# A graph layer on 100,000 nodes: three more blocks are read again before the late scatters, and their late rows are patched in

## The reference, cut to what matters

```python
h = maximum(layernorm(x), 0)                     # x: 100000 nodes x 64
z = concatenate([h[src], h[dst], edge_attr], -1) # 25000 edges x 160
e = sigmoid(z @ W_f + b_f) * softplus(z @ W_s + b_s)
message = segment_sum(e, src, 100000)            # scattered sum into the nodes
mean, var = message.mean(0), message.var(0)      # over all nodes, per feature
normed = (message - mean) * rsqrt(var + 1e-5) * gamma + beta
out = x + h + normed
```

## Time and profile before

| what | value |
|---|---|
| runs | 1060.89, 1058.82 and 1062.35 us; median 1060.89 |
| profiled execution | 1058.33 us |
| its span, first to last instruction | 1056.6 us |
| busy, share of the span | PE 60%, DVE 69%, ACT 51%, POOL 69% |
| DMA over the span | 176.07 MB, mean 167 GB/s |

### The profile page before, as it was taken

One profiled execution on the slowest core, in us unless ns is written; L12 is line 12 of the kernel. 1 busy time (PEld: TensorE's weight loads), 2 busy tenths in 40 slices (PEclk: granted clock), 3 DMA queues, 4 the chain that ended last, 5 costly groups with the idle time before them and its releaser, 6 DMA issues. The chain is left out here.

```text
span 1056.6 us, 11040 instructions
## 1 busy us (share of the span) xinstructions
PE 633.3 (60%) x2470; PEld 454.9 (43%) x2470; DVE 733.0 (69%) x1544; ACT 539.4 (51%) x1178; POOL 731.9 (69%) x652
## 2 busy tenths in 40 slices
PE   0474666666556676655666666766656699944232
PEld 0242445454445464444454444544434589710000
DVE  2884675757575776756677665776766658799687
ACT  1263655555555565645466454664545564533332
POOL 6777777777777877777877777887878753240700
PEclk9865555555565555556555555655656679955555
DMA  8997535343434344243343424424333399899999
GB/s 316 400 383 290 126 77 124 83 119 94 108 96 106 75 87 86 56 86 58 83 87 55 86 61 81 85 56 86 70 71 60 30 353 404 297 308 427 413 405 376
DMA packets 88183, 176.07 MB, mean 167 GB/s; under 512 B 42575, under 2 KB 49299, under 8 KB 79699
## 3 DMA queue, kind: packets, MB, share of 16 engines
q1 hardware_dynamic: 35851, 115.32, 31.1%
q0 software_dynamic: 42880, 20.09, 16.0%
q10 hardware_dynamic: 9416, 40.29, 9.4%
HBM read 107.12 MB, written 68.53 MB: 166 GB/s over the span
## 5 line engine op out<-in xcount | busy, mean ns | idle before, releaser
L594 POOL DMA_INDIRECT m_buf<-in_x_dram,m_buf x384 | 367.2, 956 | 118.6 <-issue 109.1
L607 POOL DMA_INDIRECT msgs_dram<-sums,target x184 | 289.6, 1574 | 56.2 <-issue 55.8
L1171 PE MATMUL ps_all<-sums,m_last 128*128 128x64 f32 x920 | 189.4, 395 | 123.7 <-ACT m_last L1033 104.2
L1171 PEld LDWEIGHTS ps_all<-sums,m_last 128*128 128x128 f32 x920 | 181.9, 304 | 134.9 <-issue 110.8
L719 DVE TENSOR_REDUCE m_last<-late 128x24 f32<-128x1536 f32 (+1 forms) x49 | 85.3, 1741 | 87.8 <-ACT late L984 87.8
L1131 PE MATMUL ps_all<-ident,m_buf 128*128 128x128 f32 x192 | 53.2, 432 | 125.8 <-DVE m_buf L809 125.8
L1145 PEld LDWEIGHTS ps_all<-m_buf 128*128 128x128 f32 x392 | 92.1, 322 | 49.5 <-issue 49.5
L794 DVE TENSOR_TENSOR target<-moved,m_last 128x4 int32<-128x4 f32 x49 | 9.6, 196 | 146.5 <-POOLq L605 146.2
L1033 ACT ACTIVATE m_last<-m_last,one_col 128x512 f32<-128x512 f32 x196 | 107.6, 550 | 1.6
L1131 PEld LDWEIGHTS ps_all<-ident,m_buf 128*128 128x128 f32 x192 | 34.9, 217 | 158.2 <-DVE m_buf L809 137.3
L1143 PE MATMUL ps_all<-m_buf 128*128 128x512 f32 x98 | 99.8, 1121 | 0.0
(11 more groups left out here) (171 smaller groups left out, 1076.6 us busy)
## 6 DMA issues: line engine op xcount, KB each, us to landing
m_buf<-msgs_dram SPq DMA_DIRECT2D x38, 1024.0 KB, 12.1
m_buf<-in_x_dram SPq DMA_DIRECT2D x48, 512.0 KB, 5.0
msgs_dram<-y_kept SPq DMA_DIRECT2D x14, 1536.0 KB, 11.2
out_dram<-m_buf ACTq DMA_DIRECT2D x20, 1024.0 KB, 11.5
m_buf<-src_rows_dram SPq DMA_DIRECT2D x47, 256.0 KB, 4.1
y_spill_dram<-y_kept ACTq DMA_DIRECT2D x19, 512.0 KB, 2.8
y_kept<-y_spill_dram SPq DMA_DIRECT2D x8, 1024.0 KB, 12.8
m_buf<-in_x_dram,m_buf POOLq DMA_INDIRECT x392, 2.5
```

What stands on the lines that cost most here:

```text
L594: pool.indirect_dma_start(xg[:, n % G_SLOTS, 2 * j + c, :], None, x, bass.IndirectOffsetOnAxis(ap=ids[:, c, n * TILES + j:n * TILES + j + ...
L607: pool.indirect_dma_start(msgs, bass.IndirectOffsetOnAxis(ap=target[:, n % UNROLL, j:j + 1], axis=0), comb[:, n % COMB_SLOTS, j, :], None, ...
L1171: pe.matmul(ps_c[:, j, :], same_of(b, j, j + 1)[:, 0, :], msg_of(g)[:, b, :], start=(b == 0 and not begun), stop=(b == j), skip_group_chec ...
```

## The change

The three blocks behind the held ones (13, 14 and 15) are treated as the held ones are: their late rows are patched into `out` after their stores. For that

- `order` takes blocks 15 down to 10 after block 24, in place of 10 up to 15, so that blocks 15, 14 and 13 are positions 9, 10 and 11;
- `list_targets` counts a late row as one to be patched from block 13 on (`first_patched`), and makes a second list, `late_add`: such rows go to their dump row, the others to their target; the late scatters use this list;
- SP loads three y blocks ahead (`Y_AHEAD` = 3), then waits for the end of the scan on PE only, and issues the re-reads 0, 1 and 2; the wait for the late scatters and the rest rows stand before re-read 3. Y load 3 + k now follows re-read k;
- POOL waits for the stores of positions 0 to 11 before the patches, where it waited for 0 to 8.

```diff
-Y_AHEAD = 4
+Y_AHEAD = 3
+PATCHED = 3
@@ stage_one
+    at.dump_row, at.dump_late = dump_row, dump_late
@@ stage_two
+    late_add = keep("late_add", [P, LATE_TILES], I32)
+    to_dump = keep("to_dump", [P, LATE_TILES])
-    order = held + [NB - 1] + list(range(SPILLED_BLOCKS, NB - 1 - M_BUFS)) + list(range(SPILLED_BLOCKS))
+    order = held + [NB - 1] + list(range(SPILLED_BLOCKS, NB - 1 - M_BUFS))[::-1] + list(range(SPILLED_BLOCKS))
-    first_held = BLOCKS[held[0]][0]
+    first_patched = BLOCKS[held[0] - PATCHED][0]
@@ sync
-        sp.wait_ge(late_added, 16 * LATE_TILES)
-        sp.wait_ge(block_crossed, M_BUFS + 2)
-        sp.dma_start(m_rest[:, :], msgs[P * N_ROWS:NODES, :]).then_inc(rest_loaded, 16)
+        sp.wait_ge(block_crossed, NB)
         for k, i in enumerate(in_ring[M_BUFS:]):
+            if k == PATCHED:
+                sp.wait_ge(late_added, 16 * LATE_TILES)
+                sp.dma_start(m_rest[:, :], msgs[P * N_ROWS:NODES, :]).then_inc(rest_loaded, 16)
             r0, n = BLOCKS[order[i]]
             sp.wait_ge(stored[buf_of(i)], 16 * stores_of(in_ring[k]))
             sp.dma_start(m_buf[:, buf_of(i), 0:n, :], m_rows[:, r0:r0 + n, :]).then_inc(m_loaded[buf_of(i)], 16)
@@ gpsimd, list_targets
-            pool.tensor_scalar(late_row[:, :], late_row[:, :], first_held - 0.5, None, ALU.is_gt
+            pool.tensor_scalar(late_row[:, :], late_row[:, :], first_patched - 0.5, None, ALU.is_gt
+            for k in range(LATE):
+                of_k = slice(k * TILES, (k + 1) * TILES)
+                ins = pool.tensor_tensor(to_dump[:, of_k], at.dump_late[:, k - 1, :] if k else at.dump_row[:, :],
+                                         late_node[:, of_k], ALU.subtract)
+            ins.then_inc(add_steps, 1)
+            pool.wait_ge(list_steps, 9)
+            pool.wait_ge(add_steps, 1)
+            pool.tensor_tensor(to_dump[:, :], to_dump[:, :], late_row[:, :], ALU.mult).then_inc(add_steps, 1)
+            pool.wait_ge(add_steps, 2)
+            pool.tensor_tensor(to_dump[:, :], to_dump[:, :], late_node[:, :], ALU.add).then_inc(add_steps, 1)
+            pool.wait_ge(add_steps, 3)
+            pool.tensor_copy(late_add[:, :], to_dump[:, :]).then_inc(add_listed, 1)
@@ gpsimd
         pool.wait_ge(rest_loaded, 16)
+        pool.wait_ge(add_listed, 1)
         def add_late(k):
-                    msgs, bass.IndirectOffsetOnAxis(ap=target[:, (EARLY + k) % UNROLL, j:j + 1], axis=0),
+                    msgs, bass.IndirectOffsetOnAxis(ap=late_add[:, k * TILES + j:k * TILES + j + 1], axis=0),
-        for i in range(len(held) + 1):
+        for i in range(len(held) + 1 + PATCHED):
             pool.wait_ge(stored[buf_of(i)], 16 * stores_of(i))
         for k in range(LATE):
             patch(k)
```

More of the change, by code:

```diff
@@ L1285, in stage_two @@
     list_done = sem("list_done")
+    add_steps = sem("add_steps")
+    add_listed = sem("add_listed")
     spare_listed = sem("spare_listed")
@@ L1409, in held_by @@
         return max([j + 1 for j in range(k) if banks(j) & banks(k)], default=0)
-    first_held = BLOCKS[held[0]][0]
+    first_patched = BLOCKS[held[0] - PATCHED][0]
+    assert order[len(held) + 1:len(held) + 1 + PATCHED] == list(range(held[0] - PATCHED, held[0]))[::-1]
     spare = BLOCKS[order[-1]][0]
```

## The result

The changed kernel takes 1061.86 us (median of 20 runs), the kernel before 1059.95 beside it: ratio 1.0015, 95% interval 1.0009 to 1.0021. By the ratio that is 1.6 us more (the medians alone differ by 1.9): clear of its own noise, within the 0.3% that the prediction takes for no change, and near the forecast of 1061.5. As a difference only +0.7 was forecast. The sum came out by luck: three of its terms were wrong and cancelled. Its profiled execution took 1060.37 us, with a span of 1058.6.

What follows compares the result with a forecast made beforehand. It took the transfer stream as the bound: the fill wins 1.5 us, but patches landing about 1053.0 make the span 1057.3 (+0.7), so 1059.0 profiled, plus 2.6 to the median, rounded to 1061.5 us; range 1056.5 to 1066.

Steps and rivals of the forecast that it cites:

- What bounds the kernel: Stage behind the message scan: a stream of transfers ending when its bytes are through, with room only ahead of 950 us.
- Re-read times: SP's re-reads 0, 1 and 2: issued near 931.5 (11.8 us earlier), 939.7 (about 5 earlier) and 947 (unmoved).
- The worth of the room: Unused DMA rate at 932 to 950 us: filling it wins 1.5 us, between 0 and 3.7.
- Order of reads and y loads, counted 0: SP's queue, re-reads each one y load further ahead: same bytes, 0 us, between -1 and +1.
- The list on GpSimd and the late scatters: Six more small operations, about 2 us, covered by some 20 idle; dump-row scatters 0, last scatter having 17 us to land.
- The patches: GpSimd's 12 additions into the output: first starts at 994.3, steps of 5.2 then 2.6 us, twelfth landed about 1053.0.
- the patches are now last: End of the final pass: position 24's two stores wait for the patches, going out at 1053.1 and 1053.5; span +0.7 us.
- the trace closes 0.6 behind such a landing: End of the trace: last stores land at 1056.7, the span closes 0.6 us later, at 1057.3.
- (a): Rival: last patch lands before 1050, only the fill is left: -1.5 us, 1059.4, at its bound 1057.2; chance 0.25.
- (b): Rival: patches stay slow to the end, 5.2 us each, twelfth at 1061.6: +9.3 us, 1070.2; chance 0.12.
- (c): Rival: re-reads come forward but nothing fills the room at 932 to 950: +1.4 us, 1062.3; chance 0.08.
- 7.7 for another wait: End of the kernel before: the patches had 7.7 us to spare ahead of position 24's stores, which wait for them.

Runs made afterwards that it cites:

- e3: The changed kernel with early re-reads but patches starting after position 8 as before, some late messages left out; 0.9982 of the kernel before, 1.9 us faster.
- e9: The changed kernel with one block (PATCHED = 1) in place of three and without GpSimd's own last wait; 1.0000 of the kernel before.
- e6: The changed kernel with two blocks (PATCHED = 2) in place of three and without GpSimd's own last wait; 0.9983 of the kernel before, 1.8 us faster.
- e8: The kernel before with Y_AHEAD = 3 alone; 1.0018 of the kernel before, 1.9 us slower.
- e4: The kernel before with patches waiting for the stores of positions 0 to 11, no early re-reads; 1.0035 of the kernel before, 3.7 us slower.
- e1: The changed kernel without GpSimd's own last wait for the patches, ACT still waiting for them; 0.9993 of the kernel before.
- e5: The changed kernel with two blocks (PATCHED = 2) in place of three, GpSimd's last wait kept; 1.0010 of the kernel before.
- e2: The kernel before without GpSimd's own last wait; 1.0003 of the kernel before.
- e7: The changed kernel with four blocks (PATCHED = 4) in place of three; 1.0026 of the kernel before.

## Why the forecast came out, step by step

- *What bounds the kernel.* Right for the stream up to its end, wrong beyond. "The stage is a stream of transfers and it ends when its bytes are through" held for the kernel before only because GpSimd's close lay under it, with 5.1 us to spare.
- *Re-read times.* 931.5, near 940 and 947 were forecast; 931.9, 942.9 and 948.7 came. Re-read 1 is later, since the stores it waits for got company: the second part of position 1 landed 8.9 us after its issue, not 6.1.
- *The worth of the room.* Taken as 1.5 us between 0 and 3.7; the early re-reads alone gave 1.9 (e3). Re-read 0, the one that I had moving far, gave nothing by itself (e9: 1.0000): SP then issued nothing from 935.1 until the last late scatter had landed. Re-reads 0 and 1 together gave as much as all three (e6: 0.9983).
- *Order of reads and y loads, counted 0.* By itself it costs 1.9 us (e8), outside my -1 to +1, because y load 3 then goes out at 942.0. In the change it goes out at 936.2, as before (935.9), so there the term was covered.
- *The list on GpSimd and the late scatters.* The list ended 1.6 us later, at 896.3, under cover. The last scatter landed 16.6 us after its issue, not 5.2 as before. Its 17 us of cover was just enough: re-read 3's buffer came free at 945.44 + 9.1 = 954.5, the scatters let SP go on at 954.7.
- *The patches.* First at 993.2 (forecast 994.3), last landed at 1050.9 (1053.0); steps were 4.25 us in the mean, where I had 5.2 and then 2.6: the first four were 4.3 each, the next four 5.2, the last three 4.2, 1.4 and 3.1. So I had a patch's pace right to 2 us over twelve by errors that partly cancelled, and took "the patches are now last" for a wait of ACT. The stores of position 24 did go out 0.4 us apart, at 1051.0 and 1051.5, so the first of them was held by about a microsecond.
- *The failed step* is the one after it: "the trace closes 0.6 behind such a landing". The changed trace closes 7.7 us behind the last patch and 4.1 behind the last store. I had asked what is queued on GpSimd behind the wait ahead of the patches and answered "only the patches", without reading the engine's close. I had 4.3 us between the last patch and the end of the span; 7.7 were measured. The last patch landed 2.1 us earlier than forecast, so 1.3 us of the error was left in the span (1058.6 against 1057.3). The median hides even that: I carried over 2.6 us between the profiled execution and the median, and it was 1.5 (1061.86 - 1060.37), as the kernel before came out 0.9 us lower in 20 runs than in the three shown (1059.95 against 1060.89). Together -2.1 + 3.4 - 1.1 = +0.2: the number came out by luck, with the mechanism of the end wrong. The DRAIN moved behind the stores costs 3.7 us by e4; the stream's own end came at 1054.5, not 1056.7.
- *The rivals.* (a) is nearest for the stream: it did end 1.5 us earlier. (b) and (c) did not happen. The Trainium skill's fit for GpSimd's transfers ("DMA: Bandwidth & Descriptors", Anatomy of one DMA) would give 2.1 us per patch by estimate; the changed trace has 10.9 to 32.9.

## What to carry to other kernels

Before work is moved later on an engine with time to spare, read when that engine's program closes, its DRAIN included, and not only when others need its results: here 5.1 us of cover stood where I had counted 7.7 for another wait, and the pieces don't show in a chain of waits. If another engine already waits for GpSimd's last transfers, its own last wait can go. Here the close then ended 4.6 us behind the last landing in place of 7.5; that was worth 2 to 3 us where the close was last (e1 against the change, e6 against e5) and nothing where it was covered (e2). In a stage that is full of transfers, what counts is megabytes in the gaps ahead of it: 0.72 MB more in the first 30 us (e3) went with 1.9 us less, 0.81 MB less (e8) with 1.9 us more, and none (e9) with no change.

## What was not expected of the hardware

GpSimd's closing DRAIN took 7.26 us in all eight traces in which GpSimd had itself waited for its transfers. In the four without that wait it waited for them and ended 4.6 or 4.7 us after the last landing. What those microseconds are spent on was not tried.

The last patch's landing follows the first one's start only in part: starts of 980.4, 984.6, 988.9, 993.2 and 998.9 gave last landings of 1043.8, 1047.2, 1050.4, 1050.9 and 1052.7 (before, e9, e5, the change, e7). Up to 988.9 most of a later start comes back at the end, beyond it only a quarter. The mean steps of the first, third, fourth and fifth of these were 4.85, 4.55, 4.25 and 4.03 us. That the later ones gain because more of them fall near or behind the end of the reads is likely: in the changed kernel the last re-read landed at 1047.2, and the patches tenth to twelfth at 1046.4, 1047.8 and 1050.9, steps of 1.4 and 3.1 us, where the kernel before, whose patches were all in before its last re-read landed, had 5.2. It was not tested by itself, and the first four steps were shorter too (4.3 us, before 4.7 to 5.3).
